# A graph-attention kernel: one TensorE block is given out in four pieces instead of two, and the tables of turns are rewritten

## The reference

```
h = relu(layernorm(x));  x = x + L0(h)   # 4 heads of 64 features, masked attention, elu
h = relu(layernorm(x));  x = x + L1(h)   # mlp 256->512, unmasked attention (512), mlp 512->256, masked attention (256)
h = relu(layernorm(x));  x = x + L2(h)   # one head, mask or identity, elu
h = relu(layernorm(x));  x = x + L3(h)   # one head, masked, relu
# attention in each: e[i,j] = leaky_relu(s_i + s_j), masked; a = softmax(e over j); out = a @ (h @ W)
```

## Time and profile before

| | before |
|---|---|
| median of 3 runs | 2958.04 us |
| the profiled execution: its time | 2958.04 us |
| its span in the trace | 2956.2 us |
| TensorE matmul busy | 2880.2 us (97%) |
| VectorE busy | 2440.6 us (83%) |
| ScalarE busy | 2317.2 us (78%) |
| GpSimd busy | 210.9 us (7%) |
| blocks of L621 passes in TensorE's order | 132 |

### The profile page before, as it was taken

The page is one execution under the profiler, slowest core; times in us unless marked ns, Lnnn a source line. Parts: engine busy times, 40 slices in busy tenths (PEclk is TensorE's granted clock), DMA queues, the critical chain, the costliest instruction groups (busy, mean ns, idle before and its releaser), DMA issues. The chain is left out here.

```text
span 2956.2 us, 66974 instructions
## 1 busy us (share of the span) xinstructions
PE 2880.2 (97%) x25624; PEld 2625.3 (89%) x25624; DVE 2440.6 (83%) x7049; ACT 2317.2 (78%) x6303; POOL 210.9 (7%) x410
## 2 busy tenths in 40 slices
PE   7999999999999999999999999999999999999997
PEld 7889988899988899888999888998889998999986
DVE  6888888888888888888888888888888888888866
ACT  6678778878778787788787787877787877887776
POOL 2000000000000000000000000000000000000000
PEclk9999999999999999999999999999999999999999
DMA  2000000000000000000000000000000000000000
GB/s 79 9 16 2 16 16 16 16 2 16 16 16 16 16 2 16 16 16 15 8 10 16 15 16 16 2 16 16 16 16 9 9 16 16 16 16 2 2 1 29
DMA packets 16367, 42.06 MB, mean 14 GB/s; under 512 B 5296, under 2 KB 6832, under 8 KB 16048
## 3 DMA queue, kind: packets, MB, share of 16 engines
q1 hardware_dynamic: 16048, 37.77, 3.6%
HBM read 20.99 MB, written 16.78 MB: 13 GB/s over the span
## 5 line engine op out<-in xcount | busy, mean ns | idle before, releaser
L585 PE MATMUL bank<-hw,R 128*128 128x257 f32 x3072 | 698.5, 383 | 2.2 <-ACT hw L1085 2.2
L585 PEld LDWEIGHTS bank<-hw,R 128*128 128x128 f32 x3072 | 569.0, 190 | 86.0 <-issue 7.3
L795 DVE SCALAR_TENSOR_TENSOR R<-bank,E,mask_ne 128x512 f32<-128x512 f32 x640 | 456.2, 742 | 3.5 <-PE bank L573 1.3
L1250 POOL TENSOR_TENSOR rs<-ve,mhalf 128x4 f32<-128x4 f32 x128 | 134.6, 1052 | 2690.3 <-DVE ve L747 2052.8
L1047 ACT ACTIVATE Z<-x,nm,rs 128x256 f32<-128x256 f32 x512 | 278.0, 592 | 45.9 <-DVE x L1012 32.4
L516 PE MATMUL bank<-wfc_hi,oThi 128*128 128x256 f32 (+1 forms) x1024 | 303.9, 297 | 5.0 <-DVE oTlo L874 2.9
L516 PE MATMUL bank<-wfc_hi,oTlo 128*128 128x256 f32 (+1 forms) x1024 | 289.6, 283 | 0.0
L516 PE MATMUL bank<-wfc_lo,oThi 128*128 128x256 f32 (+1 forms) x1024 | 289.4, 283 | 0.0
L621 PE MATMUL bank<-hw,R 128*64 128x65 f32 x8192 | 270.3, 224 | 6.2 <-DVE R L795 6.0
L621 PEld LDWEIGHTS bank<-hw,R 128*64 128x64 f32 x8192 | 250.7, 138 | 27.7 <-issue 8.0
L1070 ACT COPY Z<-bank 128x258 f32<-128x258 f32 (+1 forms) x512 | 184.7, 372 | 55.7 <-PE bank L516 54.3
(11 more groups left out here) (262 smaller groups left out, 8339.8 us busy)
## 6 DMA issues: line engine op xcount, KB each, us to landing
x<-in_x_dram SPq DMA_DIRECT2D x32, 512.0 KB, 3.4
out_dram<-x SPq DMA_DIRECT2D x32, 512.0 KB, 2.6
R<-in_adj_dram SPq DMA_DIRECT2D x2, 512.0 KB, 5.8
Z<-in_L_gnn_mlp_w_dram SPq DMA_DIRECT2D x2, 512.0 KB, 5.5
O<-in_L_gnn_W_fc_dram SPq DMA_DIRECT2D x1, 1024.0 KB, 6.8
R<-in_L_gnn_W_dram SPq DMA_DIRECT2D x1, 256.0 KB, 4.0
R<-in_L_gnn_W_hand_dram SPq DMA_DIRECT2D x1, 256.0 KB, 6.6
rowt<-in_L_gnn_W_dram SPq DMA_DIRECT2D x1, 256.0 KB, 4.6
```

The source lines that it names most:

```text
L585: ins = e.matmul(bk[:, 0:257], P[:, j, i * 128:(i + 1) * 128], hw[:, j, 0:257], start=(j == 0), stop=(j == NBLK - 1))
L795: e.scalar_tensor_tensor(P[:, t, :], bank_of(b, "row", p)[:, :], m["E"][:, 1, h, j:j + 1], mask[:, j, :], ALU.max, ALU.mult).then_inc(up(" ...
L1250: e.tensor_tensor(m["rs"][:, :], m["ve"][:, :], mhalf[:, :], ALU.pow).then_inc(up("rs", b))
```

## The change

Two things. In the head blocks the `yield` comes after each j and no longer after every second one, so that head h has four steps of 16 passes and not two of 32: 8 more steps for each batch on TensorE. And the strings of `TURNS` are written anew for all engines. TensorE's cycle has 112 digits for 104; the cycles of VectorE (150) and ScalarE (136) keep their length and change their order, GpSimd's and SyncE's cycles stay. No instruction is added or taken away on any engine. The diff, with the strings cut:

```
@@ -67,58 +67,58 @@
 TURNS = {
     "pe": (
...
-        ("2221100111010010101102201122122002112102222222111111111100112211002211211221111200021111111221221222"
-         "1111"),
+        ("2221100111010010101102201122221020102110022222021211011110110111221100022112212101111020000121111112"
+         "122212221111"),
...
@@ -623,8 +623,7 @@
                     ins.then_inc(up("att0", b))
-                    if j % 2:
-                        yield
+                    yield
```

More of the change, by code:

```diff
@@ L69 @@
     "pe": (
-        ("wwww00ww000000w0000ww0w0w000w011w0ww1w11w1ww1000000ww00001w000w0001w11220010000000000001122001001000"
-         "0111200020000002001100000121111121001000101011011220000000111111111211221100212000011101211110220111"
-         "11110001001001111"),
-        ("2221100111010010101102201122122002112102222222111111111100112211002211211221111200021111111221221222"
-         "1111"),
[L75 to L80, removed]
+        ("wwww00ww0000000w00000ww00001w10w0000ww0000w1www111ww00ww00001000011w000w000w111100102000000000121001"
+         "1111002010000011111000000020202001100000112111211020100001102120100110002210101121111112122210102120"
+         "00211100211211102222110111110001001011011"),
@@ new lines @@
+        ("2221100111010010101102201122221020102110022222021211011110110111221100022112212101111020000121111112"
+         "122212221111"),
+        ("5353445444433334443554355544544534545533555335544444444444343435533435533454534534444453333454444445"
+         "5545545454344344342323322323234432443443432324332424444432333233323432323223344223244423432343333342"
+         "2242333333434443434433333223311222211212123321333232321132232331333112221222132221221222111331122133"
+         "2323322221311132212232223332323223112222120011010001112212202121012012011200222202101211111111010010"
+         "1001000220000112121222111001000110111000021100100200120200000000010111000110001000002220000000001100"
+         "0000011112112000000111101010001000011110011101001001111010100100000"),
@@ L81 @@
     ),
     "dve": (
[L83 to L96, removed]
+        ("wwwwwwwww00w0w00000000000000ww0000001w0100000w00w000000wwww00100w00100111000101w01111000w00000000100"
+         "1010010w010010011000002100200100000001101w1110001111111100000010001000000000201001210102222122002111"
+         "2121002001002111101111102011002010111202011121111122201101012111111111121102022201112200200212102201"
+         "101001000"),
@@ new lines @@
+        ("2122222221122202022111212201100001110221000020120012202211110211211222112201210201101010111111112211"
+         "12111111111101000022201110022220010100211122122222"),
+        ("4555555354545555535445544543355433444435345334555444534435345454455453453454354344444344344334555444"
+         "3344443343444434433554544335553534345333544454555554344344444444444224333344334243332324222422323423"
+         "4433423433343332224322443344322343343333232233433443332322233333323234443334224442232342242343343443"
+         "4334332333323333211232323322133212223132331121123131222322221211211323133233222322222232122121211222"
+         "1233322212222211331123221331133112123113122323323323221122222222220022111212122101110120000200121201"
+         "2210100211122112011120011121101201210110001211011000001210211201101020001011112001110000000200011002"
+         "0200000000001120100000120000001001000100110100000100111110200111110202000010100000000000000012012001"
+         "112100110001101101100100200001110001111110102010101001111010000000"),
@@ L97 @@
     ),
     "act": (
[L99 to L111, removed]
@@ new lines @@
+        ("wwwwwww0000w00www00w00wwww0wwww1wwww1101w11w0w00ww1www1ww1w0000w0000100www22w01002w000000w0020000000"
+         "0100020000002000010000101000200020101011020101000200000100101010002100001001100001001000111111100100"
+         "021010111101001100010112111010110000001101120112110001110101110100"),
+        ("0200221112120112020221211021220222001122202112222122112121221212111220222122111122121211121211111202"
+         "121212212221120222111011211112112122"),
+        ("3335345543445454535554545545534553334555545534455545444555454554445455545454544443545554455444444535"
+         "4545555445534455554443444454554433343455334224424244344244324433442424233444442433442434334334344433"
+         "3434432344433434333434443243343334344343443434433444233343243333334323422423432313131312311332323223"
+         "3313311223333133223331322232323332222233233212323322232222323323222331233233322333322313223322122322"
+         "2222331111313120220002221222002211202212200122220221121202211211211222122111112011122121121121012211"
+         "2212021021221221120020000110010102010100122110000201202010001001100000000100001001102100011110011100"
+         "1010110002101110000110000200000110100000101000010002011001000101011110110020011011001100001010111011"
+         "1110100110100000001010110000"),
@@ L112 @@
     ),
     "pool": (
-        ("wwwww0wwwwwwwwww1ww0ww00"),
+        ("wwwwww0wwwwwwwww1ww0w0w0"),
         ("1222"),
-        ("45535444233132202101001"),
+        ("45535444233312201010012"),
     ),
@@ L120 @@
         ("21"),
-        ("10544322310"),
+        ("54043221130"),
     ),
```

## The result

The changed kernel takes 3037.48 us (median of 3 runs, 3036.89 to 3041.1) against 2958.04 us: the ratio is 1.0271, 95% interval 1.0248 to 1.0294. The forecast was 3016 us with a range of 2982 to 3036 us. The direction and the place of most of the loss were right; the size was too small, by 21 of 79 us, and the time lies 1.5 us outside the range.

A forecast was written before the change was run, and what follows sets the result against it. TensorE was taken as the bound. 54 us for 25 cycles (2.17 us each) plus 4 us at start and end, 58 us on 2958.04 us, gave 3016 us (chance 0.76); the 8-in-10 range was 2982 to 3036 us.

The forecast's parts named there:

- TensorE is the bound, and the blocks are the loss: TensorE, busy 2880.2 of 2956.2 us, sets the time; 231 more head blocks there cost 55.4 us.
- 0.24 us for each block: Price of a head block (L621) on TensorE beyond its passes: 0.09 us at the entrance, 0.14 at the exit, taken as 0.24.
- The mode rule: Changing the tiling mode drains TensorE, so the price goes with the number of head blocks, not their length.
- (a): Ahead of transpose L561 of the last scores, TensorE's wait for VectorE's `entry` goes: -0.27 us a cycle.
- (b): At the start of the unmasked attention, TensorE's wait for the low part of P goes: -0.19 us a cycle.
- (c): At the sums (L516 with hsr), TensorE's wait for VectorE's split grows from 0.41 to 1.12 us: +0.71 a cycle.
- Other waits of the cycle 0: TensorE's remaining cycle waits (turned hT, row of layer 1's scores) keep their order or are taken over later: 0.
- Start and end: half of the block price, 4 us: 31 more blocks outside the cycles cost 7.4 us; half counted, 4 us, as part falls into TensorE's idle time.
- (E): Rival: no change, within 0.2% (6 us), being (B) with every hidden wait gone too; chance 0.02.
- (B): Rival: finer steps remove TensorE's waits, as VectorE can run ahead; +18 us, 2976 us; chance 0.10.
- (C): Rival: faster, short blocks not paying 0.24 us, so only removed waits count; up to -33 us, 2925 us; chance 0.03.
- (D): Rival: slower still, TensorE's single blocks wait for VectorE's P in cycles and end strings; 3034 to 3041 us; chance 0.09.

## Why the prediction was off, step by step

- **TensorE is the bound, and the blocks are the loss.** Right. The other engines' busy time moved by less than 0.5%, and the kernel with three blocks more and nothing else lost 24.5 us.
- **0.24 us for each block.** The two terms in it were right (0.09 and 0.15, and both vanish with the 128-column tile). A third was missing: where L516 follows the block, its second pass is 0.10 us late. So the term was mis-sized there: 0.34 us by the rows, 0.33 us by the run. In TensorE's order 7 of the 12 blocks of a cycle stand ahead of L516, and 2 of 4 before, so this adds 5 x 0.10 = 0.5 us to a cycle. (What the late pass costs behind blocks that another shape follows was not worked out.)
- **The mode rule.** The Trainium skill ("TensorEngine Tiling (Array Packing)", Key Properties) says that a change of tiling mode drains TensorE. This case agrees: a block of 16 passes pays as much as one of 96, and without a change of tile there is no price.
- **(a) the wait at the transpose goes.** Right in the changed kernel (0.32 us from the mlp to the block, 0.62 on to the transpose, no wait). The cause that I gave, `entry`, was right too, since moving it removes that wait in the kernel before.
- **(b) 0.19 us at the unmasked attention goes.** Wrong, a step that failed. The 0.31 us is there in every cycle of both kernels, and twice a cycle in the changed one (1004.86 to 1005.17 above). So it comes with the change of shape from L585 to L516; I had read it as a wait for data. Nothing was gained there, and one more such place came in.
- **(c) 1.12 us of wait at the sums.** 0.97 us on the row, and the sums 3.31 us behind the transpose for 3.37. The chain was read rightly.
- **Other waits of the cycle 0.** Not quite. The wait of the row (L573) went and about as much came at a transpose (L561); those for P (L621) went. Of TensorE's waits in 24 cycles, before (233.3 to 2396.5 us):

```profile
PE bank L573 <- ACT E L1079: 6.2, 24, 0.3
PE bank L621 <- DVE R L795: 3.5, 8, 0.4
PE bank L516 <- DVE hsr L810: 3.3, 16, 0.2
```

and after (238.8 to 2457.6 us):

```profile
PE bank L516 <- DVE hsr L809: 23.4, 24, 1.0
PE bank L561 <- DVE tm L768: 7.8, 24, 0.3
```

The 24 cycles are 2163.2 and 2218.8 us, 2.32 us more each; 2.17 was forecast. The errors in it (blocks too cheap by 0.5 us, (b) by 0.19, against waits that vanished unforeseen) nearly cancel. That is luck in part.
- **Start and end: half of the block price, 4 us.** This is the step that failed, and it makes 18 of the 21 us that were missing: 21.9 us. I had read from the idle time there (7% and 5% of TensorE) that a price could hide in it. The 31 blocks cost 31 x 0.24 = 7.4 us, up to 10.5 at 0.34; the other 11 to 14 us are waits of the new order of all engines. In the end TensorE's waits at the sums rose from 2.4 to 4.7 us, at L537 (for ScalarE) from 3.0 to 5.1, and at L673 (L674 before, for VectorE) from 0.4 to 3.1, while L573, L561 and L585 gave back 3.6 together. The largest single one is new:

```profile
2916.03 0.60 PE L585 MATMUL bank<-hw,R 128*128 128x257 f32 x2
2919.19 0.36 PE L516 MATMUL bank<-HAhi,oThi 128*128 128x258 f32 x1 [2.56 <-DVE oTlo L887]
```

At the same place of the kernel before:

```profile
2838.86 5.37 PE L585 MATMUL bank<-hw,R 128*128 128x257 f32 x24
2843.88 0.47 PE L516 MATMUL bank<-HAhi,oThi 128*128 128x258 f32 x1
```

In the old end 24 passes of a masked attention, 5.0 us, stand right ahead of the unmasked attention and cover VectorE's chain to the low part of P; in the new one 2 passes do. That the cover makes this wait is read from the orders and the rows, and was not tested. I had looked through one cycle of the new order step by step, but not through the end strings, which are four batches long. Idle time in a stretch is a sign that chains set its length, and so that a new order can lengthen it; here it was no reserve.
- **The range.** Its lower end in the forecast, 3000 us, does not follow from the bound of (c): -1.12 us in 25 cycles is -28, which gives 2988. And rival (E) as described, (B) with every hidden wait gone, is 2965 us, 7 us above the kernel before and not within 6. Neither decides anything, as the time came out above.
- **The rivals.** (B) and (E) are out in sum, yet their mechanism is real: joining head 1's blocks gained nothing, so the fine steps do pay for part of themselves in the cycle they were written for. (C) is out by the run with three blocks more. (D) had the size and one of the places, a further stop in the end strings, at 9% and with its upper half outside the range. Its mechanism isn't what the traces show: in the changed kernel's end no head block waits for P.

## What to carry to other kernels

Where one shape of matmul uses another column tile, count its blocks in TensorE's order: here each costs 0.24 us at its two ends for 16 to 96 passes, and 0.34 us with the late second pass where the split products of L516 follow. Before a long distance between two starts is taken for a wait, look whether the same change of shape shows it everywhere; only what goes beyond that is a wait. A table that orders all engines is one thing: its start, its repeating part and its end added up independently here, but inside a part a step moved on one engine, or a wait shortened by itself, was paid back at the next wait (of five such trials three gave next to nothing, and two lost 23 and 104 us). Stretches with idle time are where a new order has to be followed step by step: here they took 22 us of the 79 for 31 of the 231 blocks.

## What the runs showed that I had not expected

- The distance from the first to the second pass of a stretch of L516 depends on what stood ahead: 0.20 us behind a 128-column head block, 0.22 behind a 64-column one and 0.31 behind L585, where 0.12 is usual. Behind 128-column blocks the first pass starts early by as much, so only the one behind the 64-column block is a price.
- 8 passes with 128 weight columns and 65 moving ones take 0.112 us each, nearly the 0.12 us of passes with 258 moving columns; 16 passes with 64 weight columns on alternating column halves take 0.029 us each.
- One engine's exponential moved six steps back cost 81 us, more than all 231 blocks, though no instruction was added. Up to about half of it can be TensorE's clock, which fell to 0.98 as the waits grew.
